# Two products per query preparation in place of three, with the rotary swap on the vector engine

## The chip, the cores and the metric

One core of one Trainium2 chip runs the whole kernel. The metric is device time in microseconds (us), the median of three runs. The engines are PE (TensorE: matmuls; PEld is its weight load), DVE (VectorE), ACT (ScalarE), POOL (GpSimd) and SP (SyncE, which here only issues DMAs). Each engine executes its own instructions in order and waits on semaphores.

## The reference

One transformer block on 2048 tokens of width 256: low-rank attention with rotary positions, then eight experts of which each token uses two. Only the attention's queries change. For each of 16 heads a query has 128 plain and 64 rotary features:

```
q = _rms_norm(x @ w_qa, q_a_norm_w) @ w_qb        # 96 latent features -> 16 heads x (128 + 64)
rotate_half(x): stack((-x[1::2], x[::2]))          # neighbours swapped, one of them negated
q_rope = q_rope * cos + rotate_half(q_rope) * sin
scores = (q_nope . k_nope + q_rope . k_rope) / sqrt(192), causal, softmax, times v
```

The cosines and sines repeat after 32 features, so the two members of a swapped pair do not share an angle.

## The kernel before

The kernel has three stages: `prepare` (norms, latent features, keys, weights folded together), `attend`, and `experts`. In `prepare` the plain part of the query weights is multiplied into the key weights, so that a head's query has 64 plain features and 64 rotary ones and fills 128 partitions. All float32 products are made from a high and a low part: three matmuls for each product.

`attend` works through 32 pairs of (two heads, a group of 512 queries): `PAIRS`, for each head pair the query groups 3, 1, 2, 0 (for the first head pair 0, 1, 2, 3). Each head of a pair is an item, and an item is cut into units of two key tiles: 320 units. One loop of rounds drives all engines. In round r:

- PE computes the scores of unit r (`scores`, L1141, six matmuls of up to 512 columns), between them some products whose row maxima are wanted for a later item (`maximum`, L1113), now and then a broadcast of an item's maxima (`shift_rows`, L1121), in some rounds a product of the query preparation (`query_products`, L1101), and at the end the weighted values of unit r-2 (`weigh`, L1156 to L1160).
- ACT takes the exponentials of unit r (L969, or L973 for units on the diagonal) and writes the start values of unit r+2 into the score bank (`seed`, L960). Both wait for each other through two score banks.
- POOL makes the low part of unit r's exponentials (`low_parts`, L912 and L918). `weigh(r)` waits for it, two rounds later.
- DVE takes the maxima (L1031, L1028), spreads an item's maxima (L1041), seeds one unit of each item (L1049) and empties the output bank after each item (`evacuate`, L1057). The first `weigh` of the next item waits for that.

The query preparation of pair p starts at round `PREP_ROUND[p]`, here called its round 0, and takes the next ones too. Before, three products are made, in rounds 0, 1 and 2, each into one of three work banks that the maxima use as well:

- product 0: head 0, plain features on partitions 0 to 63, rotary on 64 to 127; ACT copies the plain half (L935), DVE multiplies the rotary half by the cosines into `qf` (L1006);
- product 1: the same for head 1 with the halves exchanged;
- product 2: the rotary features of both heads once more, from weights with neighbours swapped and negated. DVE multiplies it by the sines in its bank (L1009) and adds it to the cosine parts, one sum for each head (`query_sum`, L1019, one operand from the bank and one from SBUF).

Then ACT rounds each head's query to its high part (`query_high`, L942, behind the exponentials and seed of round 2) and POOL makes the low part (`query_low`, L904, behind `low_parts` of round 2). ACT's exponentials of round 3 are queued behind L942, and POOL's low part of round 3 behind L904.

The three sets of weights are built in `prepare` (`moves`, eight pieces on ACT and eight on DVE; then stored to HBM in `store_query_weights`), and loaded for each head pair by SP. SP also loads the cosines and sines of each pair (`turn_by`).

Of the kernel before, what the change touches and what calls it, by code (L numbers as in the profile page):

```python
# [66 lines left out]
PT_RING, SHIFTS, Q_SLOTS, MAXIMA = 4, 4, 3, 4  # L67
# [25 lines left out]
PREP_AT = {r + n: (p, n) for p, r in enumerate(PREP_ROUND) for n in range(4)}  # L93
ITEM_MAX_AT = {FIRST_UNIT[i] - AHEAD: i for i in range(NI)}
assert len(SHIFT_AT) == len(ITEM_MAX_AT) == NI and len(PREP_AT) == 4 * len(PAIRS)
# [10 lines left out]
def seen_by(n):  # L106

    use = WORK_ORDER[n]
    return {"max": "v", "shift": "a", "q": "va"}[use[0]] if use[0] != "q" or use[2] < 2 else ""


SEEN = {e: [0, *itertools.accumulate(e in seen_by(n) for n in range(len(WORK_ORDER)))] for e in "av"}


# [15 lines left out]
def adaln_block_kernel(nc, x, w_qa, q_norm, w_qb, w_kva, kv_norm, w_kvb, w_o, w_gate, wi_0, wi_1, wo, c, wmod,  # L130
# [10 lines left out]
    with stack:  # L141
# [11 lines left out]
        turnstile = sb(stack, "turnstile", [P, 1])  # L153

# [14 lines left out]
        wq_dram = nc.dram_tensor("wq_parts", (2, NP, QL, 3 * P), F32, kind="Internal").ap()  # L169
# [6 lines left out]
def prepare(nc, sb, sem, k):  # L176

    bank, lat, ident, modc, gates, neg_half = k["bank"], k["lat"], k["ident"], k["modc"], k["gates"], k["neg_half"]
    turnstile = k["turnstile"]
# [3 lines left out]
    with ExitStack() as own:  # L183
# [16 lines left out]
        wa = sb(own, "wa", [P, KD, QL + KVL + DR])  # L200
        crep = sb(own, "crep", [P, KD, P])

        wq_hi = sb(own, "wq_hi", [QL, NP, 3 * P], F32R)
        wq_lo = sb(own, "wq_lo", [QL, NP, 3 * P], F32R)
# [5 lines left out]

        wv_t = sb(own, "wv_t", [P, H, KVL])
# [6 lines left out]
        qminus = sb(own, "qminus", [QL, 1])  # L218
# [13 lines left out]
        ld_o, ld_a, ld_rows, consts, wq_out = sem("ld_o"), sem("ld_a"), sem("ld_rows"), sem("consts"), sem("wq_out")  # L232
        ones_ok, qscale_ok, silu_c, crep_ok = sem("ones_ok"), sem("qscale_ok"), sem("silu_c"), sem("crep_ok")
# [41 lines left out]
        moves = []  # L275
# [14 lines left out]
        def abs_view(w, g, hd):  # L290

            at = 0 if hd == 0 else P + DR
            return w[:, 4 * g:4 * g + 4, at:at + KVL], side_of(("absorb", g))[0:QL, :].rearrange(
                "p (j two n) -> p j two n", two=2, n=KVL)[:, :, hd, :]
# [12 lines left out]
        def sync(sp):  # L307
# [22 lines left out]
            sp.dma_start(wov, k["w_o"].rearrange("(h p) n -> p h n", p=P)).then_inc(ld_o, 16)  # L330

# [60 lines left out]
        def scalar(act):  # L392
# [41 lines left out]
            def absorbed_high(g):  # L434
                act.wait_ge(side_mm, SIDE_AT["absorb", g] + 1)
                act.wait_ge(qscale_ok, 2)
# [4 lines left out]
            def rotary_weights(those):  # L441
                act.wait_ge(ld_qb, 16)
                act.wait_ge(qscale_ok, 2)
                for at, e, of, minus in those:
                    act.activation(pair_cols(wq_hi, at, e), of, ACT.Copy, scale=(qscale, qminus)[minus][:, 0:1]).then_inc(wqh_ok, 1)
# [40 lines left out]
            rotary_weights(moves[0:4])  # L486
# [9 lines left out]
            rotary_weights(moves[4:8])  # L496
# [15 lines left out]
        def vector(dve):  # L512
            dve.memset(norms[KVL:, 1:2], 1.0).then_inc(ones_ok, 1)
            dve.memset(norms[0:KVL, 2:3], 1.0).then_inc(ones_ok, 1)

# [35 lines left out]
            def rotary_low(first, last):  # L551
                for n, (at, e, of, minus) in list(enumerate(moves))[first:last]:
                    dve.wait_ge(wqh_ok, n + 1)
                    hi = pair_cols(wq_hi, at, e).bitcast(F32)
                    dve.scalar_tensor_tensor(out=pair_cols(wq_lo, at, e), in0=of, scalar=(qscale, qminus)[minus][:, 0:1], in1=hi,
# [63 lines left out]
            dve.tensor_scalar(qminus[:, :], qnw[:, :], -SCALE, None, ALU.mult).then_inc(qscale_ok, 1)  # L619
# [29 lines left out]
            rotary_low(4, 8)  # L649
# [139 lines left out]
def attend(nc, sb, sem, k, before):  # L789

    bank, lat, ident, wq_dram, values = k["bank"], k["lat"], k["ident"], k["wq_dram"], k["values"]
    ident16, mask16 = k["ident16"], k["mask16"]
# [4 lines left out]
    with ExitStack() as own:  # L797
# [3 lines left out]
        shift = [sb(own, "shift_01", [P, 2, BW])]  # L801

        q_hi, q_lo = [], []
        for n in range(2):
            q_hi.append(sb(own, f"q_hi_{n}", [P, 2, BW], F32R))
            q_lo.append(sb(own, f"q_lo_{n}", [P, 2, BW], F32R))
        ones_r = sb(own, "ones_r", [P, P], F32R)
        nmx = sb(own, "nmx", [P, 2, BT])
        sb(own, "gap_condition", [P, 56])

        wq = [sb(own, "wq_pair_hi", [QL, 3 * P], F32R)]
        q_hi.append(sb(own, "q_hi_2", [P, 2, BW], F32R))
        q_lo.append(sb(own, "q_lo_2", [P, 2, BW], F32R))
        pt_lo = [sb(own, "pt_lo_0", [P, 2, BW], F16)]
        sb(own, "gap_hi", [P, P])
        wq.append(sb(own, "wq_pair_lo", [QL, 3 * P], F32R))
        pt = [sb(own, f"pt_{n}", [P, 2, BW]) for n in range(2)]
        pt_lo.append(sb(own, "pt_lo_1", [P, 2, BW], F16))
        sb(own, "gap_lo", [P, P])

        shift.append(sb(own, "shift_23", [P, 2, BW]))
        sb(own, "gap_picked", [P, P])

        pt += [sb(own, f"pt_{n}", [P, 2, BW]) for n in range(2, PT_RING)]
        pt_lo += [sb(own, f"pt_lo_{n}", [P, 2, BW], F16) for n in range(2, PT_RING)]
        spread = [sb(own, "spread_1", [P, BT, P], F32R)]

        spread.insert(0, sb(own, "spread_0", [P, BT, P], F32R))
# [5 lines left out]
        q_turned = sem("q_turned")  # L834
# [15 lines left out]
        def wait_seen(eng, n):  # L850

            use = WORK_ORDER[n]
            if use[0] == "q" and use[2] == 2:
                eng.wait_ge(q_sum, 2 * use[1] + 2)
# [3 lines left out]
        def shift_of(item, half):  # L858
            at = item % SHIFTS
            return shift[at // 2][:, at % 2:at % 2 + half, :]  # L860
# [903 lines left out]
```

## Time and profile before

| | |
|---|---|
| median of 3 runs | 1176.46 us (1174.42 to 1178.78) |
| the profiled execution | 1178.33 us, its span 1176.4 us |
| PE busy | 1114.3 us, 95% of the span |
| DVE busy | 818.9 us, 70% |
| ACT busy | 791.4 us, 67% |
| POOL busy | 699.2 us, 59% |

The span runs from the first to the last instruction; the time includes a little around it. Up to about 100 us the kernel prepares and ramps up, attention ends near 940 us, and the experts follow. A matmul's row lists when it starts and how long it lasts; successive matmuls overlap, so that what one costs is the distance between two starts. A row of the timeline marked x2 or x3 merges instructions that follow each other.

### The profile page before, as it was taken

To read this page: it belongs to the slowest core of one execution; us is meant where nothing else is said; L and a number is where in the kernel's file an instruction comes from. 1 tells how busy PE (TensorE), PEld (TensorE's weight loads), DVE (VectorE), ACT (ScalarE), POOL (GpSimd) and SP (SyncE) were. 2 spreads that over 40 slices of the span, in tenths; PEclk is the share of its full clock that TensorE was granted. 3 is DMA by queue.
4 is the path that set the end of the run, shared out by engine and by line. 5 is a ranking of instruction groups with operands and counts; after the bars stand their busy time and mean duration, and the time that the engine had idled before them with its cause. 6 is when DMAs were issued, how large, how long until landed. Compare 5 with 4: busy or idle time off the path is not lost. (4 is left out here: it accounts for less than half of the span.)

```text
span 1176.4 us, 27725 instructions
## 1 busy us (share of the span) xinstructions
PE 1114.3 (95%) x11356; PEld 930.9 (79%) x11356; DVE 818.9 (70%) x1825; ACT 791.4 (67%) x1104; POOL 699.2 (59%) x579
## 2 busy tenths in 40 slices
PE   5769999999999999999999999999999788999997
PEld 4747788888888888888888888888887687989886
DVE  3778767676767777676767778677676566675776
ACT  3737777877778787778778787877877543333232
POOL 1436776877777677877676776868777662130000
PEclk9889999999999999999999999999999989999999
DMA  9430100010002000100100020010000050000000
GB/s 241 111 116 17 32 20 9 12 48 20 20 2 65 2 20 26 41 20 2 54 12 20 1 65 15 6 48 20 19 2 2 15 166 1 1 19 1 19 18 18
DMA packets 58126, 39.60 MB, mean 34 GB/s; under 512 B 8113, under 2 KB 57329, under 8 KB 57841
## 3 DMA queue, kind: packets, MB, share of 16 engines
q1 hardware_dynamic: 56608, 33.81, 10.3%
q10 hardware_dynamic: 1392, 4.03, 1.3%
q8 instruction: 90, 1.47, 0.5%
q14 instruction: 36, 0.29, 0.1%
HBM read 33.37 MB, written 4.46 MB: 32 GB/s over the span
## 5 line engine op out<-in xcount | busy, mean ns | idle before, releaser
L912 POOL TENSOR_TENSOR pt_lo<-pt 128x1024 f16<-128x1024 f32 x192 | 370.4, 1940 | 182.1 <-ACT pt L969 181.8
L1031 DVE TENSOR_REDUCE gates<-bank 128x1 f32<-128x512 f32 x384 | 261.6, 689 | 147.8 <-PE bank L1113 144.9
L960 ACT ACTIVATE pair<-shift 128x1024 f32<-128x1024 f32 x256 | 263.5, 1029 | 12.5 <-ACT pt L973 0.7
L969 ACT ACTIVATE pt<-pair 128x1024 f32<-128x1024 f32 x192 | 196.0, 1021 | 110.0 <-PE pair L1141 109.3
L1156 PEld LDWEIGHTS bank<-values,pt 128*128 128x128 bf16 x2176 | 196.8, 98 | 80.4 <-issue 52.5
L1156 PE MATMUL bank<-values,pt 128*128 128x65 f16 x2176 | 235.2, 195 | 6.2 <-DVE lat L1057 5.5
L1158 PE MATMUL bank<-values,pt 128*128 128x64 f16 x2176 | 231.8, 192 | 0.0
L1160 PE MATMUL bank<-values,pt_lo 128*128 128x65 f16 x2176 | 230.8, 194 | 0.0
L918 POOL TENSOR_TENSOR pt_lo<-pt 128x512 f16<-128x512 f32 (+3 forms) x256 | 178.3, 723 | 46.4 <-ACT pt L973 46.3
L1158 PEld LDWEIGHTS bank<-values,pt 128*128 128x128 bf16 x2176 | 202.0, 98 | 0.0
L1160 PEld LDWEIGHTS bank<-values,pt_lo 128*128 128x128 f16 x2176 | 201.3, 97 | 0.0
L1028 DVE CUSTOM_DVE_ANT_0 bank<-bank,mask 128x128 f32<-128x128 f32 (+3 forms) x256 | 126.1, 498 | 55.3 <-PE bank L1113 50.1
L973 ACT ACTIVATE pt<-pair 128x512 f32<-128x512 f32 (+3 forms) x256 | 109.7, 436 | 45.7 <-PE pair L1141 32.0
L1141 PE MATMUL pair<-q_hi,kt_b_hi 128*128 128x512 f32 (+1 forms) x320 | 130.9, 409 | 0.0
L1141 PE MATMUL pair<-q_hi,kt_a_hi 128*128 128x512 f32 (+1 forms) x320 | 130.6, 408 | 0.0
L1113 PE MATMUL bank<-kt_a_hi,q_hi 128*128 128x512 f32 (+2 forms) x320 | 117.1, 370 | 4.5 <-DVE qf L1019 1.8
L1113 PE MATMUL bank<-kt_b_hi,q_hi 128*128 128x512 f32 (+2 forms) x320 | 117.6, 370 | 0.2 <-DVE gates L1028 0.2
L1141 PE MATMUL pair<-q_hi,kt_b_lo 128*128 128x512 f32 (+1 forms) x320 | 117.4, 367 | 0.0
L1141 PE MATMUL pair<-q_lo,kt_b_hi 128*128 128x512 f32 (+1 forms) x320 | 117.1, 366 | 0.0
L1141 PE MATMUL pair<-q_hi,kt_a_lo 128*128 128x512 f32 (+1 forms) x320 | 116.9, 365 | 0.0
L1141 PE MATMUL pair<-q_lo,kt_a_hi 128*128 128x512 f32 (+1 forms) x320 | 116.8, 365 | 0.0
L904 POOL TENSOR_TENSOR q_lo<-qf,q_hi 128x512 fp32r<-128x512 f32 x64 | 84.4, 1341 | 14.2 <-ACT q_hi L942 12.5
(222 smaller groups left out, 2291.4 us busy)
## 6 DMA issues: line engine op xcount, KB each, us to landing
turn_by<-rope_cos_by_feature SPq DMA_DIRECT2D x64, 128.0 KB, 3.0
turn_by<-rope_sin_by_feature SPq DMA_DIRECT2D x64, 128.0 KB, 3.0
xs<-in_L_attn_x SPq DMA_DIRECT2D x4, 512.0 KB, 12.1
lat<-in_L_attn_w_o SPq DMA_DIRECT2D x1, 2048.0 KB, 9.5
xs_again<-in_L_attn_x SPq DMA_DIRECT2D x1, 2048.0 KB, 7.9
out<-xs_again SPq DMA_DIRECT2D x4, 512.0 KB, 2.8
lat<-in_L_attn_w_qb ACTq DMA_DIRECT2D x1, 1152.0 KB, 12.4
wq_parts<-wq_hi SPq DMA_DIRECT2D x1, 1152.0 KB, 7.3
```

The lines of the kernel that those rows point to most:

```text
L912: pool.tensor_tensor(out=pt_lo[at][:, :, :].rearrange("p a n -> p (a n)"), in0=full, in1=cut(full), op=ALU.subtract).then_inc(low_ok, 1)
L918: pool.tensor_tensor(out=pt_lo[at][:, half, live(u, half):], in0=full, in1=cut(full), op=ALU.subtract).then_inc(low_ok, 1)
L960: act.activation(s_pair[u % 2][:, :, :], shift_of(item, 1).to_broadcast([P, 2, BW]), ACT.Copy).then_inc(seeded["a"], 1)
L969: act.activation(pt[at][:, :, :], s_pair[u % 2][:, :, :], ACT.Exp).then_inc(exp_done, 1)
L973: act.activation(pt[at][:, half, live(u, half):], s_pair[u % 2][:, half, live(u, half):], ACT.Exp).then_inc(exp_done, 1)
L1028: dve.tensor_tensor_reduce(out=of, in0=of, in1=mask16[:, BW - n * P:], scale=1.0, scalar=LOWEST, op0=ALU.add, op1=ALU.max, accum_out=to).t ...
L1031: dve.tensor_reduce(out=to, in_=of, axis=AXX, op=ALU.max).then_inc(work_seen["v"], 1)
L1113: pe.matmul(work_of(w)[:, 0:cols], q, kt_hi[h][:, part * BW:part * BW + cols], start=True, stop=True).then_inc(work_done, 1)
L1141: last = pe.matmul(to, keys[a], q[b], start=False, stop=(m == 2), skip_group_check=True)
L1156: pe.matmul(to, cut(pt[at][:, half, mine]), with_one, start=(u == FIRST_UNIT[item] and half == 0 and t == 0), stop=False, skip_group_check ...
L1158: pe.matmul(to[:, 0:KVL], cut(pt[at][:, half, mine]), low_values, start=False, stop=False, skip_group_check=True)
L1160: last = pe.matmul(to, pt_lo[at][:, half, mine], with_one, start=False, stop=end, skip_group_check=True)
```

## The change

- Two products in place of three. Product 0 now holds the rotary features of both heads (head 1 on partitions 0 to 63, head 0 on 64 to 127), product 1 their plain features. The swapped weights are gone: four pieces in place of eight on ACT and on DVE, and a third less to store and load.
- DVE multiplies product 0 twice, all 128 partitions: by a sign column and the sines into `by_sin`, and by the cosines into `by_cos`. In the next round it exchanges neighbouring partitions of `by_sin` with a stream shuffle, in place. In round 2 it adds, for each head, 64 partitions of `by_sin` and of `by_cos`; both operands now lie in SBUF.
- The multiplication comes ahead of the swap, so the sines' rows are exchanged too: two DMAs from HBM to HBM make `sin_swapped`, and SP waits for them ahead of the first `turn_by`.
- ACT copies both plain halves from product 1 in round 1. The preparation spans three rounds, 0 to 2; it starts in the same rounds as before.
- The ring of shift rows has three places in place of four, the SBUF layout is another, and two first uses (`ones_r` on POOL, the first item's spread on DVE) now wait until the query weights are stored. DVE builds the sign column at the start with four small instructions.

```diff
-PT_RING, SHIFTS, Q_SLOTS, MAXIMA = 4, 4, 3, 4
+PT_RING, SHIFTS, Q_SLOTS, MAXIMA = 4, 3, 3, 4
...
-PREP_AT = {r + n: (p, n) for p, r in enumerate(PREP_ROUND) for n in range(4)}
+PREP_AT = {r + n: (p, n) for p, r in enumerate(PREP_ROUND) for n in range(3)}
...
-    WORK_ORDER += [("q", *PREP_AT[_r])] if _r in PREP_AT and PREP_AT[_r][1] < 3 else []
+    WORK_ORDER += [("q", *PREP_AT[_r])] if _r in PREP_AT and PREP_AT[_r][1] < 2 else []
...
-        for at, hd in ((KVL, 0), (P, 1)):
-            moves += [(at, 0, even[:, :, hd], 0), (at, 1, odd[:, :, hd], 0)]
-        for at, hd in ((2 * P, 1), (2 * P + DR, 0)):
-            moves += [(at, 0, odd[:, :, hd], 1), (at, 1, even[:, :, hd], 0)]
+        moves = [(at, e, (even, odd)[e][:, :, hd]) for at, hd in ((0, 1), (DR, 0)) for e in range(2)]
...
+            to, of = (w.rearrange("(i e) s -> e i s", e=2) for w in (k["sin_swapped"], k["sin_t"]))
+            for e in range(2):
+                sp.dma_start(to[e], of[1 - e]).then_inc(sines_out, 16)
...
+            for n, with_sign in enumerate((1.0, -1.0)):
+                dve.memset(picked[:, 0, :].rearrange("p (i e) -> p i e", e=2)[:, :, n], with_sign).then_inc(sign_ok, 1)
+            dve.wait_ge(sign_ok, 2)
+            dve.wait_ge(consts, 8)
+            dve.tensor_tensor(out=picked[:, 1, :], in0=picked[:, 0, :], in1=ident[:, :], op=ALU.mult).then_inc(sign_ok, 1)
+            dve.wait_ge(sign_ok, 3)
+            dve.tensor_reduce(out=sign[:, :], in_=picked[:, 1, :], axis=AXX, op=ALU.add).then_inc(sign_ok, 1)
...
+                        sp.wait_ge(before["sines_out"], 32)
...
-                pool.wait_ge(before["side_mm"], before["SIDE_AT"]["gate", 0] + 1)
-                pool.memset(ones_r[:, :].bitcast(F32), 1.0).then_inc(consts_ok, 1)
...
+                    if part == 2 and p == 0:
+                        pool.wait_ge(before["wq_out"], 32)
+                        pool.memset(ones_r[:, :].bitcast(F32), 1.0).then_inc(consts_ok, 1)
...
-                    act.activation(qf[PLAIN[part], part, :], work_of(n)[PLAIN[part], :], ACT.Copy).then_inc(work_seen["a"], 1)
+                    for hd in range(2):
+                        act.activation(qf[PLAIN[hd], hd, :], work_of(n)[PLAIN[hd], :], ACT.Copy).then_inc(work_seen["a"], 1)
...
+                    dve.scalar_tensor_tensor(out=by_sin[:, :], in0=work_of(n)[:, :], scalar=sign[:, :], in1=turn_by[:, p % 2, 1, :],
+                                             op0=ALU.mult, op1=ALU.mult).then_inc(work_seen["v"], 1)
+                    dve.tensor_tensor(out=by_cos[:, :], in0=work_of(n)[:, :], in1=turn_by[:, p % 2, 0, :],
+                                      op=ALU.mult).then_inc(work_seen["v"], 1)
+
+                def query_swap(p):
+                    dve.wait_ge(work_seen["v"], SEEN["v"][WORK[("q", p, 0)] + 1])
+                    dve.stream_shuffle(by_sin[:, :], by_sin[:, :], [i ^ 1 for i in range(32)]).then_inc(q_swapped, 1)
...
-                        dve.tensor_tensor(out=qf[ROT[hd], hd, :], in0=by_sin[ROT[hd], :], in1=qf[ROT[hd], hd, :],
+                        dve.tensor_tensor(out=qf[ROT[hd], hd, :], in0=by_sin[ROT[hd], :], in1=by_cos[ROT[hd], :],
                                           op=ALU.add).then_inc(q_sum, 1)
...
+                    if item == 0:
+                        dve.wait_ge(before["wq_out"], 32)
...
-                    p, part = PREP_AT.get(r, (0, 4))
-                    if part < 3:
-                        query_turn(p, part)
+                    p, part = PREP_AT.get(r, (0, 3))
+                    if part == 2:
+                        query_sum(p)
+                    if part == 0:
+                        query_turn(p)
+                    if part == 1:
+                        query_swap(p)
```

## Rows read from the trace of the kernel before

**Rows 1.** Busy time by windows, steady attention: PE, PEld, DVE, ACT, POOL, clock, DMA.
```profile
400.00:500.00 100.00, 99.93 (x1123) 82.09 (x1120) 71.88 (x155) 79.19 (x105) 73.90 (x60) 1.00 0.09 26
```

**Rows 2.** Timeline of PE, head pair 3, query group 1: start, duration, instruction.
```profile
408.62 0.39 PE L1101 MATMUL bank<-ql_hi,wq_pair_hi 96*128 96x512 f32 x1
...
411.55 0.40 PE L1101 MATMUL bank<-ql_hi,wq_pair_hi 96*128 96x512 f32 x1
...
412.26 0.21 PE L1156 MATMUL bank<-values,pt 128*128 128x65 f16 x1
```

**Rows 3.** Timeline of PE, the rounds after it.
```profile
417.02 0.21 PE L1156 MATMUL bank<-values,pt 128*128 128x65 f16 x1
...
417.76 0.48 PE L1141 MATMUL pair<-q_hi,kt_a_hi 128*128 128x512 f32 x1
...
419.70 0.21 PE L1156 MATMUL bank<-values,pt 128*128 128x65 f16 x1
```

**Rows 4.** Timeline of POOL, same place.
```profile
412.68 1.90 POOL L912 TENSOR_TENSOR pt_lo<-pt 128x1024 f16<-128x1024 f32 x1 [3.08 <-ACT pt L969]
414.79 2.55 POOL L904 TENSOR_TENSOR q_lo<-qf,q_hi 128x512 fp32r<-128x512 f32 x2 [0.21 <-ACT q_hi L942]
...
417.27 1.92 POOL L912 TENSOR_TENSOR pt_lo<-pt 128x1024 f16<-128x1024 f32 x1
```

**Rows 5.** Timeline of ACT, same place.
```profile
414.08 1.29 ACT L942 ACTIVATE q_hi<-qf 128x512 fp32r<-128x512 f32 x2 [0.41 <-DVE qf L1019]
...
416.31 1.03 ACT L960 ACTIVATE pair<-shift 128x1024 f32<-128x1024 f32 x1
```

**Rows 6.** Timeline of DVE, same place.
```profile
407.03 0.69 DVE L1006 TENSOR_TENSOR qf<-bank,turn_by 64x512 f32<-64x512 f32 x1
...
411.75 0.69 DVE L1031 TENSOR_REDUCE gates<-bank 128x1 f32<-128x512 f32 x1 [0.23 <-PE bank L1113]
...
413.29 1.41 DVE L1019 TENSOR_TENSOR qf<-bank,qf 64x512 f32<-64x512 f32 x2
```

**Rows 7.** View of line L1041: durations min/median/max in ns.
```profile
L1041 DVE TENSOR_TENSOR spread<-ident,nmx x64: 691/693/2380, 79.7 to 924.4; 128x512 fp32r<-128x512 f32 x64
```

**Rows 8.** Timeline of DVE and POOL, two places where L1041 meets L912.
```profile
143.44 2.38 DVE L1041 TENSOR_TENSOR spread<-ident,nmx 128x512 fp32r<-128x512 f32 x1
143.38 1.89 POOL L912 TENSOR_TENSOR pt_lo<-pt 128x1024 f16<-128x1024 f32 x1 [0.70 <-ACT pt L969]
...
167.00 0.69 DVE L1041 TENSOR_TENSOR spread<-ident,nmx 128x512 fp32r<-128x512 f32 x1
165.24 4.20 POOL L912 TENSOR_TENSOR pt_lo<-pt 128x1024 f16<-128x1024 f32 x2
```

**Rows 9.** Timeline of four engines, head pair 3, query group 2.
```profile
434.90 1.89 POOL L912 TENSOR_TENSOR pt_lo<-pt 128x1024 f16<-128x1024 f32 x1 [3.65 <-ACT pt L969]
435.38 1.41 DVE L1019 TENSOR_TENSOR qf<-bank,qf 64x512 f32<-64x512 f32 x2
438.40 1.03 ACT L960 ACTIVATE pair<-shift 128x1024 f32<-128x1024 f32 x1
439.74 0.48 PE L1141 MATMUL pair<-q_hi,kt_b_hi 128*128 128x512 f32 x1
```

**Rows 10.** Timeline of DVE and PE, head pair 3, query group 3.
```profile
376.12 0.42 DVE L1057 COPY lat<-bank 128x260 f32<-128x260 f32 x1
376.60 0.20 PE L1156 MATMUL bank<-values,pt 128*128 128x65 f16 x1
```

**Rows 11.** Timeline of DVE and PE, head pair 2, query group 0.
```profile
364.93 0.42 DVE L1057 COPY lat<-bank 128x260 f32<-128x260 f32 x1
365.89 0.21 PE L1156 MATMUL bank<-values,pt 128*128 128x65 f16 x1
```

**Rows 12.** Timeline of POOL and DVE in the ramp, second query preparation.
```profile
70.06 2.51 POOL L904 TENSOR_TENSOR q_lo<-qf,q_hi 128x512 fp32r<-128x512 f32 x2 [5.51 <-ACT q_hi L942]
74.75 1.41 DVE L1019 TENSOR_TENSOR qf<-bank,qf 64x512 f32<-64x512 f32 x2
```

More of the change, by code:

```diff
@@ L108, in seen_by @@
     use = WORK_ORDER[n]
-    return {"max": "v", "shift": "a", "q": "va"}[use[0]] if use[0] != "q" or use[2] < 2 else ""
-SEEN = {e: [0, *itertools.accumulate(e in seen_by(n) for n in range(len(WORK_ORDER)))] for e in "av"}
+    return {"max": {"v": 1}, "shift": {"a": 1}, "q": {"a": 2} if use[-1] else {"v": 2}}[use[0]]
+SEEN = {e: [0, *itertools.accumulate(seen_by(n).get(e, 0) for n in range(len(WORK_ORDER)))] for e in "av"}
 def live(u, half):
@@ L153, in adaln_block_kernel @@
         turnstile = sb(stack, "turnstile", [P, 1])
+        sign = sb(stack, "sign", [P, 1])
         attn = ExitStack()
@@ L199, in prepare @@
         ht = sb(own, "ht", [P, KD, BW])
[L200 to L204, printed above, removed]
+        wq_hi = sb(own, "wq_hi", [QL, NP, 2 * P], F32R)
+        wq_lo = sb(own, "wq_lo", [QL, NP, 2 * P], F32R)
         junk = sb(own, "junk", [P, BT, QL + KVL])
@@ L209, in prepare @@
         picked = sb(own, "picked", [P, 2 * KD, P])
+        wa = sb(own, "wa", [P, KD, QL + KVL + DR])
+        crep = sb(own, "crep", [P, KD, P])
         wv_t = sb(own, "wv_t", [P, H, KVL])
@@ L290, in abs_view @@
         def abs_view(w, g, hd):
-            at = 0 if hd == 0 else P + DR
+            at = P + hd * KVL
             return w[:, 4 * g:4 * g + 4, at:at + KVL], side_of(("absorb", g))[0:QL, :].rearrange(
@@ L442, in rotary_weights @@
                 act.wait_ge(ld_qb, 16)
-                act.wait_ge(qscale_ok, 2)
-                for at, e, of, minus in those:
-                    act.activation(pair_cols(wq_hi, at, e), of, ACT.Copy, scale=(qscale, qminus)[minus][:, 0:1]).then_inc(wqh_ok, 1)
+                act.wait_ge(qscale_ok, 1)
+                for at, e, of in those:
+                    act.activation(pair_cols(wq_hi, at, e), of, ACT.Copy, scale=qscale[:, 0:1]).then_inc(wqh_ok, 1)
             def twins(b):
@@ L485, in scalar @@
             normalise(3)
-            rotary_weights(moves[0:4])
+            rotary_weights(moves)
             squares(2)
@@ L495, in scalar @@
             twins(2)
-            rotary_weights(moves[4:8])
             squares(3)
@@ L551, in rotary_low @@
             def rotary_low(first, last):
-                for n, (at, e, of, minus) in list(enumerate(moves))[first:last]:
+                for n, (at, e, of) in list(enumerate(moves))[first:last]:
                     dve.wait_ge(wqh_ok, n + 1)
                     hi = pair_cols(wq_hi, at, e).bitcast(F32)
-                    dve.scalar_tensor_tensor(out=pair_cols(wq_lo, at, e), in0=of, scalar=(qscale, qminus)[minus][:, 0:1], in1=hi,
+                    dve.scalar_tensor_tensor(out=pair_cols(wq_lo, at, e), in0=of, scalar=qscale[:, 0:1], in1=hi,
                                              op0=ALU.mult, op1=ALU.subtract).then_inc(wql_ok, 1)
@@ L859, in shift_of @@
             at = item % SHIFTS
-            return shift[at // 2][:, at % 2:at % 2 + half, :]
+            return shift[:, at:at + half, :]
         def work_of(n):
@@ L1013, in query_sum @@
+                def query_swap(p):
+                    dve.wait_ge(work_seen["v"], SEEN["v"][WORK[("q", p, 0)] + 1])
+                    dve.stream_shuffle(by_sin[:, :], by_sin[:, :], [i ^ 1 for i in range(32)]).then_inc(q_swapped, 1)
                 def query_sum(p):
-                    for part in range(2):
-                        wait_seen(dve, WORK[("q", p, part)])
-                    dve.wait_ge(q_turned, p + 1)
-                    by_sin = work_of(WORK[("q", p, 2)])
+                    if p > 0:
+                        dve.wait_ge(q_lo_ok, 2 * p)
+                    dve.wait_ge(q_swapped, p + 1)
@@ L1188, in _ @@
                     p, part = PREP_AT.get(r, (0, 3))
-                    if part < 3:
+                    if part < 2:
                         query_products(p, part)
```

90 lines of the change are left out of this document (38 added, 52 removed).

## Prediction, made before the changed kernel was run

> **What bounds the kernel now.** I read the page first: PE is busiest. Then the view of busy time by windows, for how even that is: in the steady part of attention PE is busy 99.93 of 100 us, ACT 79, POOL 74, DVE 72, at the full clock of 2.4 GHz [rows 1]. So whatever PE no longer does shortens the time, as long as nothing that PE waits for is also just in time. For that I read the timeline of each engine around one query preparation, that of head pair 3 and group 1, and looked at how long before PE's use each input was ready. Two are close. The low part of round 3 ends at 417.27 + 1.92 = 419.19 and PE weighs with it at 419.70: 0.51 us to spare [rows 3, 4]. The seed of round 5's scores ends at 416.31 + 1.03 = 417.34 and PE starts them at 417.76: 0.42 us [rows 3, 5]. The shortest interval after which PE goes on is 0.06 us (an output bank emptied at 376.54, used at 376.60 [rows 10]); for the seed I allow 0.1 us. So about 0.45 and 0.3 us are free, in the very rounds in which the change takes work from PE. PE is the bound, and POOL and ACT are one third of a microsecond behind it there.
>
> **What PE saves.** The third product is three matmuls. From the first one's start to the start of what follows is 412.26 - 411.55 = 0.71 us [rows 2] (their durations of 0.40 us overlap and would overstate it). Thirty-two preparations make 22.7 us. That is the gain if nothing else holds PE up, and the lower end: 1178.3 - 22.7 = 1155.6.
>
> **The new sums.** Count and place on DVE: before, five operations of 512 columns (two, then product 2 with two sums); after, two in round 0, the shuffle in round 1, two sums in round 2. The number is the same. The multiplication with the sign column and the shuffle have no row. From above and below: no 512-column DVE operation here takes under 0.69 us, and the worst takes 2.38 [rows 6, 7]. I take 0.7 us for both, that of all plain rows of that size: one pass over 512 columns. In round 0 the one operation of before ends at 407.03 + 0.69 = 407.72 [rows 6], and PE starts product 1, the next that needs DVE's release of that bank, at 408.62 [rows 2]: 0.9 us cover the second operation's 0.7, barely. If each took 0.2 us longer, PE would wait some 0.2 us in each place, 6 us in all.
>
> What matters is that the sums read both operands from SBUF. Before, one was in PSUM, and they took 1.41 us for two while POOL worked beside them [rows 4, 6]. L1041 is the one DVE operation in attention that reads two SBUF operands: its median is 693 ns and its worst 2380 [rows 7]. At 143.44 it starts 0.06 us after POOL's L912 and ends 0.55 us after L912's end at 145.27: it waited for all of it. At 167.00 it starts while one L912 is about to end: it takes 0.69 us and the two L912 together 4.20 in place of 3.80, so the next one stood back 0.4 us [rows 8]. One of the two engines always waits until the other's instruction is over.
>
> The Trainium skill says the same (SBUF — State Buffer, "SBUF: two separate sides": a DVE operation with two SBUF inputs and a GpSimd operation that reads SBUF take a shared pair of ports by an exclusive lock). Its page VectorE: DVE Perf Modes, in the section on the TRN2 errata, speaks for the change: a DVE operation costs 58 cycles and its columns from SBUF, 120 from PSUM, an estimate of 0.06 us less for each sum, 4 us of DVE time. The rows do not bear that out: 0.69 us from two SBUF operands [rows 7] against 1.41 for two sums with one in PSUM [rows 6]. By that page the sum below would be some 2 us lower.
>
> **Where the sums fall.** Take E, the end of the last maximum of round 2: 411.75 + 0.69 = 412.44 [rows 6]. The first sum runs from E to E + 0.70, and L912 wants to start at E + 0.24 [rows 4]. It then stands back about 0.3 us. After the first sum I see two orders:
>
> - *POOL next.* L912 runs to E + 2.45, the second sum ends 0.55 us after that, at E + 3.0 (before: 414.70, E + 2.26). That is 0.75 us later. The second L942, then L969 and L960 of round 3 are queued behind it on ACT: the seed is 0.75 later against 0.3 us free, so PE starts the scores of round 5 about 0.44 us later than before.
> - *The second sum next.* Both sums are done at E + 1.42, L912 ends 1.0 us later than before, and POOL has L904 twice and L912 behind it. It makes up its idle 0.21 [rows 4] and the 0.45 free: PE weighs 0.4 us later than before.
>
> Either way this place loses 0.4 us where it should win 0.71.
>
> The same for the other kinds of place; the order of groups repeats for each head pair, so four kinds cover pairs 4 to 28 of the 32. Group 2: L912 starts at 434.90, as the first sum ends; the second waits for it and ends at 436.79 + 0.55, against 435.38 + 1.41 = 436.79; the seed ends at 439.43 for 439.74, so + 0.34 us, or + 0.2 in the second order [rows 9]. Group 3: here DVE itself is just in time: L1057 ends at 376.54 and PE goes on at 376.60 [rows 10]; the second sum is as late as in group 2, near 0.6 us, and L1057 is behind it: + 0.59, or + 0.4. Group 0: L1057 ends at 365.35 for 365.89 [rows 11], 0.48 us free against 0.58: + 0.10, or, in the second order, the full - 0.71. Sum over 7, 6, 6 and 6 places: POOL next, 3.1 + 2.0 + 3.5 + 0.6 = + 9.2; second sum next, 2.8 + 1.2 + 2.4 - 4.3 = + 2.1. The last three places, where less is free, add 1; the two before the steady part I take as zero.
>
> **The ramp.** The second preparation's first DVE work waits for the first one's L904, which ends at 72.57; its sums end at 76.16 [rows 12]. After the change the multiplications do not write `qf` and need not wait; only the sums do, and they end at 72.60 + 1.41 = 74.0. The first maxima follow: - 2.1 us, if DVE then sets the pace, zero if not.
>
> **Edits at nothing.** Four pieces of weights fewer on ACT and DVE: PE waits at that time for other products, the chain to the output rows goes through POOL. The two DMAs for the sines are issued behind the loads of the preparation stage, and the first `turn_by` is read only in the ramp, after all of that stage: SP's transfers have that long to land. If not, the ramp moves by what is missing. `ones_r` and the first spread wait for the stored weights, which are complete earlier since the last pieces are. Shift rows, three places: a row is overwritten more than a whole item after its last use. The sign column is made while DVE waits for its first input.
>
> **Sum.** The trace does not show who is next after two DVE operations in a row, so I take the middle of 8 and 1: + 4.6 us on the profiled execution's 1178.3, 1182.9. The median is 1.9 us lower: 1181. This case's own range is 1174 to 1190.
>
> **Rivals.**
>
> 1. *The saving comes through.* The sums mostly miss POOL, or 64 partitions collide less. Then only the free time limits: group 1 saves up to 0.66, group 2 0.4, group 0 0.71, group 3 0.3: 4.6 + 2.5 + 4.3 + 1.7 = 13, with the ramp 15, so 1162; with DVE's gaps closing up as well down to 1154. For it: over half of L1041's 64 runs are undisturbed [rows 7]. Against it: they come at another point of the round, and the sums stand right where L912 starts, in each place. It decides once the second sum is less than 0.3 us late.
> 2. *The delay spreads.* A second sum 1.7 us late pushes DVE's maxima, spread and L1057 into further collisions with L904: another 0.5 us in each of 28 places, + 14 us, 1195. For it: DVE is just in time in group 3 already. It decides if L1041 of the next round is blocked as well.
> 3. *No swap gain, no loss.* The shuffle takes the lock too or needs 1.5 us. It stands in round 1, where POOL works on the short diagonal units, and costs at most the 0.1 to 0.3 us by which DVE is late there: 3 to 9 us on top, 1186.
>
> **Chances.** The case of the sum 0.5, the saving through 0.3, the delay spreading 0.12, the slow shuffle 0.08. A measurement tells about 0.5%, 5.9 us, from no change: 1170.6 to 1182.3. Of the first case a little over half lies within it, the rest above. Faster 0.30, same 0.31, slower 0.39. Range for 8 in 10: 1159 to 1194.
>
> **What the profile after would show.** L1101 in 192 matmuls in place of 288. The sums' line with a median near 0.7 and a maximum near 2.4 us, one of two long; L912 or L904 of 2.2 us beside them. PE no longer busy 99.9 of 100: waits at the scores for L960 and at the weighing for POOL's low part or L1057, some 0.7 to 1.1 us in each preparation. If instead both sums take 0.69 us and PE stays at 99.9, the prediction is wrong by the whole saving. If PE waits for the work banks in rounds 0 and 1, the two multiplications or the shuffle are what I priced too low.

## The result, and the profile after

The changed kernel takes 1198.66 us (median of 4 runs, 1197.63 to 1200.01) against 1176.04 us of the kernel before in the same comparison: a ratio of 1.0191 [1.0175, 1.0208], 1.9% slower. Forecast were 1181 us and a range that ended at 1194. The profiled execution took 1197.63 us, 19.3 more than that of before.

Page of the kernel after, busy time and the row of granted clock:

```profile
span 1195.8 us, 27473 instructions
...
PE 1110.6 (93%) x11260; PEld 921.2 (77%) x11260; DVE 862.1 (72%) x1856; ACT 787.3 (66%) x1100; POOL 714.0 (60%) x579
...
PEclk8989999999999999999999999999999989999998
```

PE does have less work: 96 matmuls fewer. DVE is busy 862 us instead of 819, though its operations of 512 columns are as many as before. One window of steady attention, to be held against [rows 1] (400 to 500 us):

```profile
400.00:500.00 100.00, 95.79 (x1091) 78.29 (x1090) 76.47 (x154) 76.17 (x105) 74.91 (x61) 0.98 0.09 25
```

Where 99.93 of 100 us were busy at full clock, 95.79 are now, at 0.98 of it. So PE waits. What for, by the view of PE's waits (total us, times, longest). First the wait for the output bank in the kernel before, then two waits of the kernel after:

```profile
PE bank L1156 <- DVE lat L1057: 5.5, 5, 1.8
...
PE bank L1164 <- DVE lat L1061: 22.2, 23, 2.3
...
PE pair L1149 <- ACT pair L962: 5.7, 14, 0.8
```

L1164 is the first weighing (L1156 before), L1061 the emptying of the output bank (L1057 before), L1149 the scores, L962 the seed. The wait for the output bank is the large one, 22.2 us where it was 5.5. DVE's operations by line, durations min/median/max in ns, first and last start:

```profile
L1021 DVE TENSOR_TENSOR qf<-by_sin,by_cos x64: 683/690/2379, 66.5 to 924.3; 64x512 f32<-64x512 f32 x64
...
L1045 DVE TENSOR_TENSOR spread<-ident,nmx x64: 691/693/2380, 75.6 to 944.0; 128x512 fp32r<-128x512 f32 x64
...
L1014 DVE STREAM_SHUFFLE by_sin<-by_sin x32: 709/794/803, 65.8 to 921.0; 128x512 f32<-128x512 f32 x32
...
L1007 DVE SCALAR_TENSOR_TENSOR by_sin<-bank,sign,turn_by x32: 740/750/754, 64.4 to 915.2; 128x512 f32<-128x512 f32 x32
```

The sums read 690 ns at the median and 2379 at the worst, as [rows 7] showed for the spread. In 28 of the 32 preparations one of the two is long (all but 0, 1, 2 and 30, counted from 0): the timelines below merge the two into 2.99 us, where they took 1.41 [rows 6].

**One place.** Timelines of head pair 3, group 3, the place of [rows 10]. DVE:

```profile
373.31 2.99 DVE L1021 TENSOR_TENSOR qf<-by_sin,by_cos 64x512 f32<-64x512 f32 x2
...
377.35 0.15 DVE L1040 TENSOR_REDUCE nmx<-gates 128x4 f32<-128x12 f32 x1
377.54 1.69 DVE L1045 TENSOR_TENSOR spread<-ident,nmx 128x512 fp32r<-128x512 f32 x1
379.15 0.41 DVE L1061 COPY lat<-bank 128x260 f32<-128x260 f32 x1
```

POOL (L909 is `low_parts`, L901 `query_low`):

```profile
373.83 1.92 POOL L909 TENSOR_TENSOR pt_lo<-pt 128x1024 f16<-128x1024 f32 x1 [2.57 <-ACT pt L971]
375.72 2.96 POOL L901 TENSOR_TENSOR q_lo<-qf,q_hi 128x512 fp32r<-128x512 f32 x2
378.64 4.19 POOL L909 TENSOR_TENSOR pt_lo<-pt 128x1024 f16<-128x1024 f32 x2
```

PE:

```profile
377.00 0.28 PE L1121 MATMUL bank<-kt_b_hi,q_hi 128*128 128x256 f32 x1
379.62 0.20 PE L1164 MATMUL bank<-values,pt 128*128 128x65 f16 x1 [2.34 <-DVE lat L1061]
```

Read them in order of time. L909 ends at 373.83 + 1.92 = 375.75; the second sum ends at 373.31 + 2.99 = 376.30, 0.55 us later: it had waited for all of L909. Then the maxima, and the spread starts at 377.54, inside L901 (375.72 to 378.68). It ends at 379.23, again 0.55 us after POOL's end: it waited as well. L1061 stands behind it on DVE, though it does not need the spread's result; it ends at 379.56, and PE goes on at 379.62. Counted from the start of the scores of round 2 (369.43 before, 370.87 after), the bank is empty after 8.69 us instead of 7.11: 1.58 us later.

**The clock.** Windows of the same kernel, at this place and at the same place of head pair 5. The last three numbers of a row are the granted clock, the busy share of DMA and its GB/s:

```profile
377.20:379.60 2.40, 0.08 (x1) 0.00 (x0) 2.36 (x6) 2.37 (x3) 2.40 (x3) 1.00 0.52 148
379.60:384.00 4.40, 4.38 (x33) 3.59 (x33) 1.23 (x7) 1.48 (x3) 3.23 (x2) 0.61 0.16 42
384.00:390.00 6.00, 6.00 (x96) 5.39 (x96) 3.79 (x8) 5.07 (x8) 4.64 (x5) 1.00 0.02 5
...
597.00:599.45 2.45, 0.12 (x1) 0.00 (x0) 2.41 (x6) 2.42 (x3) 2.45 (x3) 1.00 0.52 142
599.45:603.85 4.40, 4.40 (x62) 3.78 (x63) 2.66 (x9) 2.80 (x4) 3.86 (x3) 1.00 0.16 44
```

Both times PE has stood still for 2.34 us. At pair 3 it then works 4.4 us at a granted clock of 0.61, most of the stretch at the lower level of 1.2 GHz, and gets 33 matmuls through; at pair 5 it gets 62 through at full clock. So the same idle time costs about 1.5 us more in some places. All six places of group 3 counted below have the same 2.34 us; in four the granted clock of the next 4.4 us is 0.61 to 0.64, in two it is 1.00, and the trace of kernel 8 below has the same four and the same two.

**The sum over places.** The distance between the scores of round 2 of successive preparations, after minus before, gives what each place costs. The 25 places counted are those of pairs 5 to 29, counted from 0; 7, 6, 6 and 6 are their numbers in groups 1, 2, 0 and 3:

| us in each place | group 1 | group 2 | group 0 | group 3 |
|---|---|---|---|---|
| forecast, order "POOL next" | +0.44 | +0.34 | +0.10 | +0.59 |
| measured | +0.42 | +0.32 | +0.43 | four of 2.97 to 3.15, two of 1.56 and 1.59 |
| sum over 7, 6, 6, 6 places, forecast | 3.1 | 2.0 | 0.6 | 3.5 |
| the same, measured | 3.0 | 1.9 | 2.5 | 15.4 |

That is 22.8 us against 9.2. With what lies ahead of the scores of round 2 of head pair 1, group 3 (- 4.4), that place itself (+ 0.4), and what follows the places counted (+ 0.7), it makes 19.5. The last scores of attention come 19.6 us later than before, and the profiled executions differ by 19.3.

### The profile page after: what moved, and what is told of

Same layout as the page of the kernel before. It is cut to its first block and busy times, and to the rows that moved or that the text cites. A ratio compares the mean times of both kernels' runs of the same rounds, so it can differ in the third digit from the quotient of the medians.

```text
span 1195.8 us, 27473 instructions
## 1 busy us (share of the span) xinstructions
PE 1110.6 (93%) x11260; PEld 921.2 (77%) x11260; DVE 862.1 (72%) x1856; ACT 787.3 (66%) x1100; POOL 714.0 (60%) x579
## 3 DMA queue, kind: packets, MB, share of 16 engines
q10 hardware_dynamic: 1392, 4.03, 1.3%
## 5 line engine op out<-in xcount | busy, mean ns | idle before, releaser
L909 POOL TENSOR_TENSOR pt_lo<-pt 128x1024 f16<-128x1024 f32 x192 | 376.7, 1970 | 193.5 <-ACT pt L971 192.7
L1164 PEld LDWEIGHTS bank<-values,pt 128*128 128x128 bf16 x2176 | 197.7, 99 | 95.9 <-issue 53.8
L962 ACT ACTIVATE pair<-shift 128x1024 f32<-128x1024 f32 x256 | 263.4, 1029 | 11.9
L1164 PE MATMUL bank<-values,pt 128*128 128x65 f16 x2176 | 236.8, 195 | 22.7 <-DVE lat L1061 22.2
L915 POOL TENSOR_TENSOR pt_lo<-pt 128x512 f16<-128x512 f32 (+3 forms) x256 | 178.8, 723 | 46.8 <-ACT pt L975 46.7
L1149 PE MATMUL pair<-q_hi,kt_a_hi 128*128 128x512 f32 (+1 forms) x320 | 132.8, 415 | 3.0 <-ACT pair L962 3.0
L1149 PE MATMUL pair<-q_hi,kt_b_hi 128*128 128x512 f32 (+1 forms) x320 | 130.9, 409 | 2.7 <-ACT pair L962 2.7
L1121 PE MATMUL bank<-kt_b_hi,q_hi 128*128 128x512 f32 (+2 forms) x320 | 119.8, 377 | 1.4 <-DVE gates L1033 1.3
L1121 PE MATMUL bank<-kt_a_hi,q_hi 128*128 128x512 f32 (+2 forms) x320 | 116.9, 369 | 4.0 <-DVE gates L1030 1.5
L1149 PE MATMUL pair<-q_hi,kt_a_lo 128*128 128x512 f32 (+1 forms) x320 | 118.8, 371 | 0.0
L1149 PE MATMUL pair<-q_lo,kt_a_hi 128*128 128x512 f32 (+1 forms) x320 | 118.4, 370 | 0.0
L1149 PE MATMUL pair<-q_hi,kt_b_lo 128*128 128x512 f32 (+1 forms) x320 | 117.4, 367 | 0.0
L1149 PE MATMUL pair<-q_lo,kt_b_hi 128*128 128x512 f32 (+1 forms) x320 | 117.1, 366 | 0.0
L901 POOL TENSOR_TENSOR q_lo<-qf,q_hi 128x512 fp32r<-128x512 f32 x64 | 93.2, 1478 | 9.0 <-ACT q_hi L944 9.0
## 6 DMA issues: line engine op xcount, KB each, us to landing
lat<-in_L_attn_w_kvb ACTq DMA_DIRECT2D x1, 1024.0 KB, 11.9
```

What stands on the lines that cost most here:

```text
L909: pool.tensor_tensor(out=pt_lo[at][:, :, :].rearrange("p a n -> p (a n)"), in0=full, in1=cut(full), op=ALU.subtract).then_inc(low_ok, 1)
L915: pool.tensor_tensor(out=pt_lo[at][:, half, live(u, half):], in0=full, in1=cut(full), op=ALU.subtract).then_inc(low_ok, 1)
L962: act.activation(s_pair[u % 2][:, :, :], shift_of(item, 1).to_broadcast([P, 2, BW]), ACT.Copy).then_inc(seeded["a"], 1)
L1121: pe.matmul(work_of(w)[:, 0:cols], q, kt_hi[h][:, part * BW:part * BW + cols], start=True, stop=True).then_inc(work_done, 1)
L1149: last = pe.matmul(to, keys[a], q[b], start=False, stop=(m == 2), skip_group_check=True)
L1164: pe.matmul(to, cut(pt[at][:, half, mine]), with_one, start=(u == FIRST_UNIT[item] and half == 0 and t == 0), stop=False, skip_group_check ...
```

## The experiments

The kernel before, run beside them, had medians of 1176.82 us (the first four) and 1176.52 us (the last four). Theory: the lock between a DVE operation with two operands in SBUF and POOL's instruction, and DVE's order, which puts the output bank behind it. Rivals: the shuffle or the multiplications are the cost, or DVE's longer busy time is, or the new layout and the shorter shift ring are.

| kernel | median us | ratio to before |
|---|---|---|
| 1 before, sums from SBUF | 1209.42 | 1.0278 [1.0244, 1.0312] |
| 2 after, sums with one input | 1160.77 | 0.9864 [0.984, 0.9887] |
| 3 after, sums first | 1161.68 | 0.9875 [0.9852, 0.9899] |
| 4 after, bank emptied first | 1181.56 | 1.0051 [1.0035, 1.0067] |
| 5 after, 3 and 4 together | 1156.54 | 0.9822 [0.9785, 0.986] |
| 6 as 5, both parts of the query early | 1161.91 | 0.9872 [0.9833, 0.9911] |
| 7 as 3, multiplications wait | 1164.45 | 0.9888 [0.9848, 0.9929] |
| 8 after, no shuffle | 1194.34 | 1.0147 [1.011, 1.0185] |

And what the places of each kind cost against before, read as above:

| us in each place | group 1 | group 2 | group 0 | group 3 |
|---|---|---|---|---|
| 1 | +0.79 | +1.04 | +1.27 | +1.26 to +1.55 |
| 2 | -0.71 | -0.47 | -0.65 | -0.13 |
| 3 | -0.71 | -0.47 | -0.65 | -0.13 |
| 4 | +0.42 | +0.32 | +0.43 | +0.22 |
| 5 | -0.71 | -0.47 | -0.65 | -0.34 |
| 6 | -0.37 | -0.70 | -0.37 | -0.85 |
| 7 | -0.71 | -0.49 | -0.65 | -0.14 |
| 8 | +0.42 | +0.32 | +0.43 | four of 2.94 to 3.15, two of 1.55 and 1.57 |

**1. The kernel before with its sums from SBUF.** All three products stay. The place of one operand moves; to make room for it the ring of shift rows has three places, as after the change.

```diff
-PT_RING, SHIFTS, Q_SLOTS, MAXIMA = 4, 4, 3, 4
+PT_RING, SHIFTS, Q_SLOTS, MAXIMA = 4, 3, 3, 4
...
-                        dve.tensor_tensor(out=work_of(n)[:, :], in0=work_of(n)[:, :], in1=turn_by[:, p % 2, 1, :],
+                        dve.tensor_tensor(out=by_sin[:, :], in0=work_of(n)[:, :], in1=turn_by[:, p % 2, 1, :],
...
-                    by_sin = work_of(WORK[("q", p, 2)])
```

> The kernel before, with all three products; only L1009 writes its result to SBUF, so that both operands of the two sums lie in SBUF (three shift rows make room for the tile). Lock theory (a DVE operation with two SBUF operands and a POOL operation exclude each other): here the sums start 0.6 us after L912, so the first waits 1.3 us for its end; the seed of round 5 comes about 1.1 us late against 0.3 us free, 0.8 us or more in each of 28 places, and 3 us where DVE is just in time: 1200 to 1215 us. Rival (the loss comes from the swap, the two multiplications, the layout or the shift ring): within 3 us of 1176.

1209.42 us, 33 more than before. Of the change it has the operands' place, and the shift ring with the layout that goes with it. Its sums, and two of PE's waits:

```profile
L1019 DVE TENSOR_TENSOR qf<-by_sin,qf x64: 683/690/2245, 67.6 to 935.3; 64x512 f32<-64x512 f32 x64
```

```profile
PE bank L1156 <- DVE lat L1057: 11.6, 10, 1.8
PE bank L1121 <- DVE qf L1019: 8.5, 7, 2.5
```

The same 690 ns at the median, 2245 at the worst, and PE stands behind the same bank (11.6 us, where the kernel before has 5.5) and, at the broadcast of the maxima (L1121), behind the sums themselves. There is no shuffle here, no second multiplication and no missing product, so none of these is needed for the loss. The shift ring and the layout are not told apart from the operands by this kernel; kernels 2 and 3 do it, since they keep both and are fast.

**2. Sums with one input.** Shuffles that move nothing stand where the sums stood; the kernel leaves out the addition of the cosine part.

```diff
-                        dve.tensor_tensor(out=qf[ROT[hd], hd, :], in0=by_sin[ROT[hd], :], in1=by_cos[ROT[hd], :],
-                                          op=ALU.add).then_inc(q_sum, 1)
+                        dve.stream_shuffle(qf[ROT[hd], hd, :], by_sin[ROT[hd], :], list(range(32))).then_inc(q_sum, 1)
```

> The changed kernel, with each of the two sums replaced by a shuffle of by_sin alone: one SBUF operand, same place, 64 partitions, 512 columns (the addition of the cosine part is left out). Lock theory: nothing waits, and what is left is the smaller work of PE, limited by the free time of POOL and ACT: 1157 to 1165 us. Rival (swap, multiplications, layout): still 1193 to 1200.

1160.77 us. The line of the sums is now

```profile
L1021 DVE STREAM_SHUFFLE qf<-by_sin x64: 719/743/756, 68.5 to 888.6; 64x512 f32<-64x512 f32 x64
```

Each operation is longer than an undisturbed sum (743 against 690 ns) and none is long: with one SBUF input none waits for POOL. 38 us of the changed kernel's time hang on the second input. The saving on PE was there all along: a place of group 1 is 0.71 us shorter than before, which is all of one product.

**3. Sums first.** `query_sum` ahead of the maxima of round 2, when POOL has not yet started on that round's low part.

```diff
+                    p, part = PREP_AT.get(r, (0, 3))
+                    if part == 2:
+                        query_sum(p)
                     for c in CHUNKS_AT[r]:
                         maximum(c)
                     if r in ITEM_MAX_AT:
                         item_shift(ITEM_MAX_AT[r])
-                    p, part = PREP_AT.get(r, (0, 3))
-                    if part == 2:
-                        query_sum(p)
```

> The changed kernel, with the two sums ahead of the maxima of round 2 instead of behind them, a time in which POOL waits for ACT's exponentials. Lock theory: the sums meet no POOL instruction, both take 0.69 us: 1157 to 1163 us, 12 us of it from the places (POOL's and ACT's free time limits) and 4 from the ramp. Rival (DVE's load or the swap): the same work on DVE in another order, 1193 to 1200.

1161.68 us, by a move of three lines and with the whole computation. Timelines of the place that was read above (pair 3, group 3), first DVE, then POOL:

```profile
360.55 1.57 DVE L1021 TENSOR_TENSOR qf<-by_sin,by_cos 64x512 f32<-64x512 f32 x2
...
365.38 1.39 DVE L1045 TENSOR_TENSOR spread<-ident,nmx 128x512 fp32r<-128x512 f32 x1
366.70 0.42 DVE L1061 COPY lat<-bank 128x260 f32<-128x260 f32 x1
```

```profile
359.37 2.21 POOL L915 TENSOR_TENSOR pt_lo<-pt 128x384 f16<-128x384 f32 x3
...
363.08 1.90 POOL L909 TENSOR_TENSOR pt_lo<-pt 128x1024 f16<-128x1024 f32 x1 [1.50 <-ACT pt L971]
364.93 2.98 POOL L901 TENSOR_TENSOR q_lo<-qf,q_hi 128x512 fp32r<-128x512 f32 x2
```

The sums start under the last short pieces of the round before's low part (L915, until 361.58) and are over at 362.12, 0.96 us before L909 starts. They take 1.57 us instead of 2.99, of which some 0.2 us are still waiting. L1045 still starts inside L901, and waits 0.7 us of its 1.39: it ended up between L901's two instructions. PE still waits for the bank, 0.64 us in this place and 8.4 us in 10 waits in all. That is why group 3 gains only 0.13.

**4. The bank emptied first.** Where a round has both, `evacuate` goes ahead of `item_shift`.

```diff
+                    early = r in ITEM_MAX_AT and r >= 2 and UNITS[r - 2][2] == 2
+                    if early:
+                        evacuate(r - 2)
                     if r in ITEM_MAX_AT:
                         item_shift(ITEM_MAX_AT[r])
...
-                    if r >= 2 and UNITS[r - 2][2] == 2:
+                    if r >= 2 and UNITS[r - 2][2] == 2 and not early:
                         evacuate(r - 2)
```

> The changed kernel, where a round has both, the output bank is emptied (L1061) ahead of the item's spread (L1045). Theory: in the places of group 3, 3.0 us are lost because L1061 stands behind L1045, which waits for POOL, and the idle PE then falls to half its clock; ahead of it L1061 comes 1.8 us earlier, PE idles 0.6 us and keeps its clock: about 2 us less in each of six places, 1184 to 1190 us. Rival (these places are lost to the seeds or to POOL's low part as the others are): 1196 to 1199.

1181.56 us: 17 us less than the changed kernel, more than I expected (1184 to 1190). Timelines of the same place, DVE and then PE:

```profile
372.41 2.99 DVE L1021 TENSOR_TENSOR qf<-by_sin,by_cos 64x512 f32<-64x512 f32 x2
...
376.45 0.42 DVE L1061 COPY lat<-bank 128x260 f32<-128x260 f32 x1
376.79 0.15 DVE L1040 TENSOR_REDUCE nmx<-gates 128x4 f32<-128x12 f32 x1
376.97 1.37 DVE L1045 TENSOR_TENSOR spread<-ident,nmx 128x512 fp32r<-128x512 f32 x1
```

```profile
376.93 0.20 PE L1167 MATMUL bank<-values,pt 128*128 128x65 f16 x1 [0.54 <-DVE lat L1061]
```

The sums are as slow as ever (2.99), the spread still waits, but the bank is empty before it and PE waits 0.54 us instead of 2.34. Group 3 falls from 3.1 or 1.6 us to 0.22, which is 14.1 us over six places, and the last place gives 3.8; the other kinds stay at 0.42, 0.32 and 0.43 to the hundredth. Against that, this execution reached head pair 1, group 3, 2.0 us later than the changed kernel's. It was 2.4 us later at the first scores already, and up to there the two kernels are the same: so far does the early part scatter between executions. This is also close to the case of my forecast: with group 3 not spreading, 1181.6 us, where 1181 was predicted. But it is near out of other terms than those of the forecast, as the next section says.

**5. Both.** The edits of 3 and 4.

> The sums ahead of the maxima of round 2, and the output bank emptied ahead of the item's spread. With the sums first, L1045 still meets L901 in the places of group 3 (1.39 us in place of 0.69) with L1061 behind it, and there the gain over the kernel before is 0.13 us where the others have 0.47 to 0.71. Theory: L1061 ahead of it gives 0.3 to 0.5 us back in six or seven places, 1157.5 to 1160.5 us. Rival (POOL's low part of round 3 is what limits these places): 1161 to 1162.5.

1156.54 us, 1.8% faster than before and 3.5% faster than the change as it was made. Group 3 goes from - 0.13 to - 0.34. It is 20.0 us less than before's 1176.52, where PE's whole saving was put at 22.7; some 2 of the 20 come from the ramp and not from PE. I had expected 1157.5 to 1160.5. PE's waits:

```profile
PE bank L1167 <- POOL pt_lo L909: 3.9, 8, 0.9
```

The next thing that is late is POOL's low part: 0.38 us in the places of group 3. In the changed kernel PE waited for it 0.5 us in all. Against kernel 3 the medians differ by 5 us, but the two were timed beside different runs of before and their intervals touch; the profiles differ by 1.5 us at the last unit of attention. How much more than that the fifth is worth is open.

**6. Both parts of the query early.** As 5, with L944 ahead of the exponentials and L901 ahead of the low parts in round 2.

```diff
+                    if PREP_AT.get(r, (0, 3))[1] == 2:
+                        query_high(PREP_AT[r][0])
                     if 0 <= r < NU:
                         exponentials(r)
...
-                    if part == 2:
-                        query_high(p)
```

(and the same exchange of `query_low` and `low_parts` on POOL)

> As the run with both orders, and in round 2 ACT makes the high parts (L944) ahead of its exponentials, and POOL the low parts (L901) ahead of low_parts, in the 1 to 2.5 us in which both wait for PE. Theory: the low part of round 3, which now limits groups 2, 0 and 3, comes 1 us earlier, and each place gives the full 0.7 us: 1153 to 1157 us. Rival: L944 delays the exponentials of round 2 by 0.8 us and with them POOL and the next seeds, 1160 to 1168.

1161.91 us: a miss. Groups 2 and 3 do what was expected, - 0.70 and - 0.85: there L901 is out of the spread's way. Groups 1 and 0 lose half of theirs, - 0.37 for - 0.71 and - 0.65, since exponentials and seed now stand behind L944, and PE waits for the seed, 0.14 to 0.17 us in each of the places looked at. Over the 25 places kernel 6 is still 1.0 us ahead of kernel 5. What it loses by the profiles is in the ramp, 2.3 us up to head pair 1, group 3; in the window of 60 to 120 us the granted clock is 0.80, where that of kernel 5 is 0.91. That makes 1.3 us at the last scores, of the 5.4 us between the medians; the profiled execution of kernel 5 is the slowest of its four, and where the rest lies is open. The same exchange in the places of groups 2 and 3 alone was not run.

**7. The multiplications wait.** As 3, and in `query_turn` DVE waits for the pair before's low parts, as it had to before the change.

```diff
+                    if p > 0:
+                        dve.wait_ge(q_lo_ok, 2 * p)
```

> The run with the sums first, but DVE's multiplications wait for the previous pair's low parts, as they did in the kernel before. In steady attention these are long done, so this undoes one thing alone, the earlier second preparation in the ramp. Theory (it is the ramp's gain): 2 us slower than 1161.7, 1163 to 1165. Rival (the ramp's gain comes from the smaller products, weights or the earlier store): 1161 to 1162.5.

1164.45 us, 2.8 more than kernel 3 beside other runs of before; by the ratios 1.5, and their intervals overlap, so the times alone do not show it. The traces do. The sums of the first and of the second preparation, in the changed kernel and then in kernel 7:

```profile
66.54 1.40 DVE L1021 TENSOR_TENSOR qf<-by_sin,by_cos 64x512 f32<-64x512 f32 x2
70.57 1.40 DVE L1021 TENSOR_TENSOR qf<-by_sin,by_cos 64x512 f32<-64x512 f32 x2 [0.41 <-POOL q_lo L901]
...
67.08 1.40 DVE L1023 TENSOR_TENSOR qf<-by_sin,by_cos 64x512 f32<-64x512 f32 x2
73.36 1.40 DVE L1023 TENSOR_TENSOR qf<-by_sin,by_cos 64x512 f32<-64x512 f32 x2
```

From the first to the second it is 4.03 us in the changed kernel and in kernels 3, 4, 5, 6 and 8 too (to 0.01), 6.28 in kernel 7, and 6.13 in the kernel before. That is the step of the ramp that the forecast had at 2.1.

**8. No shuffle.** A memset of one small tile stands in its place; neighbours are not exchanged.

```diff
-                    dve.stream_shuffle(by_sin[:, :], by_sin[:, :], [i ^ 1 for i in range(32)]).then_inc(q_swapped, 1)
+                    dve.memset(k["turnstile"][:, :], 0.0).then_inc(q_swapped, 1)
```

> The changed kernel with the shuffle left out (neighbours are not exchanged; a one-element write tells that the place is passed). Lock theory: the shuffle takes 0.78 us in a round in which DVE has time; without it 1195 to 1199 us. Rival (the shuffle blocks POOL or delays the banks): 1180 or less.

1194.34 us, with the places as they were in the changed kernel: + 0.42, + 0.32, + 0.43, and in group 3 the same four near 3.0 and two near 1.6. In steady attention the 0.79 us of each shuffle cost nothing. The 4 us between the medians are not in the places; the profiled execution of kernel 8 took 1198.1 us, beside 1197.63 of the changed one. I take them for the scatter between runs (the intervals of the two ratios overlap), and no experiment here settles it.

## Why the prediction was wrong, point by point

- **PE as the bound, 0.3 and 0.45 us free on the others.** Right. The seed's 0.75 us against 0.3 free was to cost 0.44 in group 1, and 0.42 was measured; group 2 had 0.34 and 0.32. In both PE also waits 0.2 to 0.3 us for the output bank just ahead of that, which the forecast did not name; the seed is the wait that ends last.
- **The saving of 22.7 us.** Right, and the change kept none of it in steady attention. In kernels 2, 3, 5 and 7 a place of group 1 is 0.71 us shorter than before, the whole of one product. The bound without waits, 1155.6, was for the profiled execution; in medians it is 1153.8, and kernel 5 comes to 1156.5.
- **The lock.** Right: the median near 0.7, the maximum near 2.4, one of two sums long in 28 of 32 places, the end 0.55 us after POOL's. Kernels 1 and 2 show it from both sides, + 33 and - 38 us. The Trainium skill's rule of the shared pair of ports (SBUF — State Buffer, "SBUF: two separate sides"), which the forecast weighed, agrees with these traces: operations with two SBUF inputs wait (690 ns alone, up to 2379 with the wait), those with one do not (719 to 756). The table in the section on the TRN2 errata of the Trainium skill's page VectorE: DVE Perf Modes, from which the forecast estimated 0.06 us less for each sum, is not borne out: undisturbed they take 690 ns, two of them 1.40 in the ramp, against 1.41 with one operand in PSUM [rows 6].
- **The order after the first sum.** Two were seen, and the middle of their sums, 8 and 1, was taken. In each of the 27 preparations 3 to 29 the first sum took 0.69 us, POOL was next, and the second sum waited; the four kinds' steps follow that order. No second sum went ahead of a waiting L909. Going by the middle cost 3.5 us.
- **Group 3, + 0.59 in each place: the step that failed.** The working took the second sum's lateness, 0.6 us, straight through to L1057, as if everything between them would only be moved. But the spread stands between (L1041, now L1045), itself with two operands in SBUF, and the shift put its start (377.54) inside L901. It waited 1.0 us (1.69 for 0.69), so that the bank was 1.58 us late and not 0.59. In four of six places PE's 2.3 us of idleness were then followed by the lower clock, another 1.5 us. Measured 15.4 us over six places for 3.5. Kernel 4 shows the first part of it by taking L1061 out from behind the spread. The rival "the delay spreads" is this mechanism; its condition, "if L1041 of the next round is blocked as well", was met, but it got a chance of 0.12 and was priced as a general loss of 0.5 us in 28 places, where it sits in six at 1.6 to 3.1 us. The forecast's own numbers led there: the second sum late by 0.6 us, the maxima behind it, and L904 on POOL at that time. (Its "pairs 4 to 28" does not fit its own 7, 6, 6 and 6: these are the numbers of pairs 5 to 29, counted from 0.)
- **The clock: no term at all.** About 6 us by the difference between 3.06 and 1.58 us (the means of the four places and of the two) in four places. The forecast saw the full clock of [rows 1] and did not ask what idle stretches would do to it. It left out this term without a reason.
- **Group 0, + 0.10.** Measured + 0.43, 1.9 us too little over six places. The bank had 0.48 us free as stated, and PE did not wait for it. It waited for the maxima behind the sums (0.21 us) and for a shift row that ACT copies behind the late second L944 (0.36 us), two users of the same lateness that the term left out.
- **The ramp, - 2.1.** Right, in size and in mechanism: from the first to the second preparation's sums it is 4.03 us in place of 6.13, and 6.28 again with the wait put back (kernel 7). The profiled execution was 4.4 us ahead at head pair 1, group 3; 2.1 of these lie ahead of the first sums already, which end at 67.94 in place of 70.03. PE's first wait, for the load of the weights `wmod`, ended at 7.95 us there and at 10.15 before, and it ends anywhere from 7.7 to 10.2 in the ten traces. How much of the 2.1 is this scatter and how much the smaller work on the weights was not tried.
- **Edits at nothing.** The multiplications were put at 0.7 us and take 0.75 and 0.68, the shuffle at 0.7 and takes 0.79. The shuffle does not show in the steps per place (kernel 8), so the rival of the slow shuffle is out for steady attention. The longer multiplications were not tried by themselves; kernels 2, 3 and 5 contain them and are fast.
- **The sum.** Middle of the orders 3.5 us too low, group 3 11.9, group 0 1.9, the place ahead of those counted 0.4; groups 1 and 2 together 0.2 too high, what lies ahead of the places 2.3, the last places 0.3: 4.6 + 3.5 + 11.9 + 1.9 + 0.4 - 0.2 - 2.3 - 0.3 = 19.5, where 19.3 was measured. That kernel 4 landed at 1181.6 is no merit of the 1181: without the group-3 loss the place-by-place sum gives about that, but out of other terms.

## What to carry to other kernels

Before an operand is moved from PSUM to SBUF, list which DVE operations read two SBUF operands and when POOL works; such an operation belongs where POOL waits or has only short pieces left, and here three lines moved made 1.9% slower into 1.2% faster. When one operation becomes late, carry the new times through its queue and ask of each one behind it whether it now starts under another engine's instruction: the six places in which one did cost 15.4 us instead of 3.5, the lower clock included. What nobody needs soon (the spread) stands behind what PE waits for (the output bank), and a forecast that finds two possible orders should name one from the timelines and price the other as a rival, not take their middle.

## What was not expected of the hardware

- Of two sums in a row the second loses to POOL's instruction that came up during the first: 2.99 us for two, of which 1.6 are waiting. The other way round, a DVE operation that waits goes ahead of POOL's next instruction: the two L901 take 2.96 us after the waiting sum, and 2.98 with a spread between them (kernel 3), where two L904 took 2.55 [rows 4]. The two engines take turns; neither finishes its queue first.
- After the same 2.34 us without a matmul the granted clock was 0.61 to 0.64 over the next 4.4 us in four places and 1.00 in two, the same ones in two kernels. What tells them apart stayed open.
- A shuffle of 128 partitions by 512 columns takes 0.79 us, of 64 partitions 0.74, and its mask 14 ns. It reads one operand and never waited for POOL.
